# A graph network layer on one Trainium2 core: moving own sums, aggregate, turn and scatter between the gathered tiles on TensorE

## The reference

```python
w = jax.nn.relu(edgefeats @ fnet_w1 + fnet_b1) @ fnet_w2 + fnet_b2
W = w.reshape(-1, nc, nc)
deg = segment_sum(ones, edge_dst); inv_deg = 1.0 / maximum(deg, 1.0)
for _ in range(NREPEATS):                                  # 2
    xj = hx[edge_src]
    m = jnp.einsum('ei,eio->eo', xj, W)
    agg = jax.ops.segment_sum(m, edge_dst, num_segments=n_nodes) * inv_deg[:, None]
    hx = _gru_cell(agg, hx, ...)
x = _layernorm(x + hx)
```

## Time and profile before

| | |
|---|---|
| time, median of 3 runs | 6458.52 us (6440.29 to 6484.48) |
| profiled execution | 6451.35 us, its span 6449.0 us |
| mean granted clock of TensorE | 0.912 |
| PE busy | 85% of the span |
| DVE busy | 69% |
| POOL busy | 57% |
| ACT busy | 52% |

### The profile page before, as it was taken

One profiled execution on the slowest core, in us unless ns is written; L12 is line 12 of the kernel. 1 busy time (PEld: TensorE's weight loads), 2 busy tenths in 40 slices (PEclk: granted clock), 3 DMA queues, 4 the chain that ended last, 5 costly groups with the idle time before them and its releaser, 6 DMA issues.

```text
span 6449.0 us, 124558 instructions
## 1 busy us (share of the span) xinstructions
PE 5491.4 (85%) x41939; PEld 4396.8 (68%) x41940; DVE 4426.8 (69%) x5962; ACT 3328.3 (52%) x5306; POOL 3653.1 (57%) x3867
## 2 busy tenths in 40 slices
PE   2888888888888888888877888888988888888887
PEld 1766666676676776666646777767777767777775
DVE  3866666666666666666656777777777777777776
ACT  1555555555555555555434555555555555555553
POOL 6355555555555555555546555555555555555553
PEclk7998999998999999999988999999999999999998
DMA  5111111111111111111111111111111111111110
GB/s 119 40 45 36 51 36 51 36 51 36 42 44 41 46 38 49 36 51 36 48 51 31 31 43 37 37 43 31 43 43 31 43 31 43 43 31 43 43 31 21
DMA packets 190346, 270.76 MB, mean 42 GB/s; under 512 B 90119, under 2 KB 158234, under 8 KB 176887
## 3 DMA queue, kind: packets, MB, share of 16 engines
q1 hardware_dynamic: 58779, 224.93, 10.4%
q0 software_dynamic: 123168, 31.78, 4.7%
q10 hardware_dynamic: 7838, 6.41, 0.4%
HBM read 202.89 MB, written 54.94 MB: 40 GB/s over the span
## 4 chain that ended last, share of the span: by engine, by line
PE 67%; issue 13%; another core or an unknown queue 10%; ACT 5%; DVE 3%; DVEq 1%; ACTq 0%; DMA 0%; SPq 0%
PE ps_all L838 40%; PE ps_all L850 8%; PE ps_all L840 6%; PE ps_all L825 4%; ACT src_hot L700 3%; PE ps_all L873 3%; PE ps_all L894 2%; PE ps_all L864 2%; ACT src_hot L704 1%; DVE shared L1303 1%; DVE fan L1263 1%; PE ps_all L880 1%; DVE xg L1311 0%; PE ps_all L899 0%
## 5 line engine op out<-in xcount | busy, mean ns | idle before, releaser
L838 PE MATMUL ps_all<-parts,src_hot 128*128 128x448 f32 x14478 | 3672.3, 390 | 245.6 <-issue 97.2
L838 PEld LDWEIGHTS ps_all<-parts,src_hot 128*128 128x128 f32 x14478 | 2848.5, 199 | 639.3 <-issue 289.3
L628 POOL DMA_INDIRECT xg<-in_x,idx x1973 | 1868.6, 947 | 1435.5 <-issue 510.8
L628 POOL DMA_INDIRECT xg<-h_rows,idx x1876 | 1770.1, 944 | 1258.6 <-issue 474.8
L1303 DVE TENSOR_TENSOR shared<-ps_all,at_hot 128x448 f32<-128x448 f32 x2413 | 1406.7, 618 | 1499.8 <-PE ps_all L840 824.2
L700 ACT ACTIVATE src_hot<-keys,neg_key 128x384 fp32r<-128x384 int16 (+1 forms) x3088 | 1687.8, 619 | 1218.7 <-remote 578.5
L1311 DVE TENSOR_REDUCE xg<-shared 128x48 f32<-128x1344 f32 (+1 forms) x772 | 1244.3, 1612 | 82.0 <-DVE shared L1303 2.3
L704 ACT ACTIVATE src_hot<-src_hot 128x1536 fp32r<-128x1536 f32 (+1 forms) x772 | 1190.0, 1541 | 71.4
L1263 DVE TENSOR_TENSOR fan<-xg,ps_all 128x1280 f32<-128x1280 f32 x784 | 1159.5, 1479 | 40.7 <-issue 19.4
L850 PE MATMUL ps_all<-fan,h_sb 128*32 128x160 f32 x12544 | 742.5, 310 | 230.3 <-issue 209.8
L840 PE MATMUL ps_all<-parts,src_hot 128*128 128x448 f32 x2413 | 909.0, 377 | 13.1 <-issue 12.8
(11 more groups left out here) (134 smaller groups left out, 1368.3 us busy)
## 6 DMA issues: line engine op xcount, KB each, us to landing
keys<-key_d SPq DMA_DIRECT2D x98, 832.0 KB
h_d<-h_sb SPq DMA_DIRECT2D x49, 1056.0 KB
h_sb<-h_d SPq DMA_DIRECT2D x49, 1056.0 KB
xg<-in_x,idx POOLq DMA_INDIRECT x1973
xg<-h_rows,idx POOLq DMA_INDIRECT x1876
ef<-in_ef_t SPq DMA_DIRECT2D x49, 420.0 KB
acc_all<-agg_t SPq DMA_DIRECT2D x1, 3161.0 KB
idx<-in_src_tiles SPq DMA_DIRECT2D x98, 32.0 KB
```

What stands on the lines that cost most here:

```text
L628: pool.indirect_dma_start(out=xg[:, buf, at, 0:C], out_offset=None, in_=rows_of, in_offset=bass.IndirectOffsetOnAxis(ap=idx[:, buf, at:at ...
L838: pe.matmul(ps_g[j], src_hot[k % 2][:, kb, j * P:(j + 1) * P], parts[:, m * WHOLE + kb, :], start=(kb == 0 and m == 0), stop=False)
```

## The change

Nothing is added to or removed from the computation, and the streams of DVE, ACT, POOL and SP stay as they are. On TensorE `gather_rows` can now do part of its tiles. In each step, hidden and the first gathered tile come directly behind products. Then follow own sums, turn or scatter where the step has them, and the other gathered tiles behind these. In step 0 one tile stands between own sums and aggregate, and the last one behind aggregate.

```diff
-            def gather_rows(rnd, s, k):
+            def gather_rows(rnd, s, k, first=0, end=SLOTS):
 
-                for j, (n, _, _) in enumerate(pe_tiles(rnd, k)):
+                for j, (n, _, _) in list(enumerate(pe_tiles(rnd, k)))[first:end]:
...
+                        if rnd == 0 and not is_last(i):
+                            hidden(rnd, i + par, 1 - par, sup + 1, k)
+                        if not is_last(i):
+                            gather_rows(rnd, s + 1, k, 0, 1)
+                        elif SIDE_FROM <= k < HPS - 1:
+                            side_gates(rnd, k)
                         if not is_first(i, par):
                             if k == 0:
                                 pe.wait_ge(s_super, sup)
                                 own_sums(rnd, sup - 1, 1 - buf, 1)
+                                if not is_last(i):
+                                    gather_rows(rnd, s + 1, k, 1, 2)
                                 aggregate(sup - 1)
...
                             own_sums(rnd, sup, buf, 0)
-                        if rnd == 0 and not is_last(i):
-                            hidden(rnd, i + par, 1 - par, sup + 1, k)
                         if not is_last(i):
-                            gather_rows(rnd, s + 1, k)
-                        elif SIDE_FROM <= k < HPS - 1:
-                            side_gates(rnd, k)
+                            gather_rows(rnd, s + 1, k, 2 if k == 0 and not is_first(i, par) else 1)
```

## The result

The changed kernel takes 6764.22 us (median of 4, 6740.61 to 6769.57) against 6449.41 us of the kernel before in the same comparison: ratio 1.0477 with a 95% interval of 1.042 to 1.0534. The forecast was 6775. The total came out within 11 us; as the experiments show, its terms did not come out nearly so well, and two large errors cancelled.

A forecast was written before the change was run, and what follows sets the result against it. TensorE and POOL were taken to hand each other the step, small products waiting for POOL's DMA runs. Terms of 2.15 and 4.5 us a supertile gave 319 us over 48 supertiles, forecast 6775 us; range 6370 to 7100, likeliest 6600 to 6900.

The forecast's parts named there:

- The bound: TensorE and POOL hand each other the step; small products are handed over only between two runs of POOL's DMAs.
- Own sums in step 0: Behind a tile they are caught by POOL's run: +1.35 us a supertile in round 0, +2.9 in round 1.
- The tile ahead: Step 0: where products are late, a tile fills lost time: -1.0 us a supertile in round 0, -0.3 in round 1.
- Own sums in step 6: Caught by POOL's run too, with only two tiles behind: +0.4 us a supertile, bound 1.25 us per caught group.
- Aggregate: Step 0: it comes later, delaying ACT's copy and step 1's `src_hot`: +1.2 and +1.4 us a supertile, bounds 0 and 3.1.
- Turn and scatter: Issued behind a tile, so DVE's adding and ACT's copy start later: +0.2 and +0.1 us a supertile.
- The sum by rounds: All terms together: +2.15 us a supertile in round 0 and +4.5 in round 1, over 48 supertiles each.
- Faster by split bursts: Rival: halved bursts of small products end the stalls before own sums, at most 272.8 us gained (6185); chance 0.22.
- No change: Rival: POOL's hand-over paces the step, so moved stalls lengthen nothing: 6450 +- 60 us; chance 0.15.
- Borders at 164 us: Rival: each border pair between small and full-width products costs 0.31 us on TensorE, giving 6940 us; chance 0.08.
- Far slower: Rival: own sums caught in nearly every group as POOL's runs join, and the clock falls: 7130 us and above; chance 0.13.

The follow-up runs named there:

- e1: Kernel before, with only own sums of step 0 moved behind hidden and one gathered tile, aggregate directly behind them: 6513.36 us, ratio 1.0081, first chip.
- e10: Kernel before, with own sums of step 0 moved behind hidden and one tile in round 0 only: 6365.61 us, ratio 0.9866, first chip.
- e2: Kernel before, with only own sums of step 6 moved behind hidden and one gathered tile: 6608.03 us, ratio 1.0228, first chip.
- e3: Kernel before, with only aggregate moved behind hidden and two gathered tiles: 6623.49 us, ratio 1.0262, first chip.
- e12: Kernel before, with only aggregate moved and POOL's indirect DMAs replaced by plain ones of the same size: 5198.8 us, ratio 1.0415, third chip.
- e4: Kernel before, with only turn and scatter moved behind hidden and one gathered tile: 6462.77 us, ratio 1.0004, first chip.
- e9: Changed kernel with POOL's indirect DMAs replaced by plain ones of the same size, against the kernel before: 5282.73 us, ratio 1.0579, second chip.
- e11: Kernel before, own sums of step 0 moved in round 0 only, POOL's runs after own sums waiting for them: 5000.69 us, ratio 1.0014, second chip.

## Why the prediction was right, and where it was not

- **The bound.** That TensorE and POOL hand each other the step held on the first chip: POOL's waits for products, with those whose releaser isn't shown, are 308 us longer in a span that is 310 us longer. It was stated as a property of the small products and POOL's DMAs; the second chip shows that it is a property of the executions on the first chip, of which the profile of before could give no hint.
- **Own sums in step 0** (+1.35 and +2.9 us a supertile). The mechanism is right, its shares were not: products of step 0 were late in 40 of 41 supertiles of round 0, not in 70%, and newly held own sums were 5 of 41 there, not 30%. In round 1 they were 40 of 41, not 65%. The step's length was read from one step: 10.3 us, where the mean of round 0 is 14.2, so the 14.2 us that I forecast for the step after the change is what it took before. After it, it takes 10.2, and step 1 takes the time instead. With tile ahead and a part of aggregate's delay this step stood for 204 us in e1, and 52 to 55 were measured: -1.9 instead of +0.95 in round 0, +3.2 for +3.3 in round 1.
- **The tile ahead** (-1.0 and -0.3 us), named as the only gain, was under-sized in round 0. e10, in which hardly any own sums of round 0 are held, has it nearly alone: -1.3% of the kernel.
- **Own sums in step 6** (+0.4 us, 38 us in all) was the step that failed: e2 measured 147 to 150 us. The bound of 1.25 us was drawn inside the step. The cost fell two steps later, where POOL's runs join and catch own sums and aggregate of step 0, so that the step takes 19.4 us, a part of them at the lower clock. I had the row of such a joined run and used it as an upper bound of the wrong term.
- **Aggregate** (+1.2 and +1.4 us, 125 us in all): mechanism right, size 169 us alone on the first chip and 254 us on the third. "Less than half" of the shift was too little as a mean, and wrong by rounds: e3 has +0.1 us in round 0, where POOL's cycle takes the delay up, and +3.4 in round 1, where own sums of step 6 are also held in 38 of 41 supertiles. Where that cycle doesn't exist, e12 has +2.3 and +3.0 us, near the upper bound of 3.1.
- **Turn and scatter** (15 us): nothing measurable, +4 us.
- **The sum by rounds** came out as +2.0 and +4.6 us for +2.15 and +4.5. With e1 to e4 known this is luck: by them the terms should have come to about -1 and +12 us. In the whole, own sums of step 6 were 110 us too small and aggregate 44, own sums of step 0 and the tile ahead 150 us too large.
- **The rivals.** Faster by split bursts: excluded in both rounds as a whole; the "issue" time in front of own sums does fall, from 272.8 to 29.8 us (of their weights from 314.2 to 103.5), but DVE's wait at its copy of own sums grew, and "issue" grew in front of products, gathered tiles and aggregate. No change: excluded. Borders at 164 us: against it speak e4 on the first chip, for scatter alone, and e9, where at most 106 us can be borders. Far slower did not come on the whole, but its mechanism, joined runs and a clock at its lower level, is what made e2.

## What to carry to other kernels

Before a group of work is moved back on one engine, follow who copies its result and what stands behind that copy: here one copy of aggregate on ScalarE blocks the next step's `src_hot`, and that alone was three quarters of the cost on chips where nothing was held. Where two engines hand each other the step, a delay is not priced within its own step; look where the other engine's runs will join. Pieces of a change that are measured one by one can add up in total and still not explain it; compare them stage by stage. And a pattern of waits that only one chip shows is no law of the kernel: two edits that gained 1.3% and 0.9% there gained nothing together on the next.

## What the runs showed of the hardware that I had not expected

The same kernel took 6450 us on one chip, 4994 us on a second and 4992 on a third. POOL's DMAs are equally long in the traces of the first two (0.94 us, 1.25 us apart), and the mean granted clocks are 0.91 and, in e11, 0.99. On the first chip small products wait for the end of POOL's run of indirect DMAs: 512 of 784 groups of products in the kernel before, with a median of 2.7 us from the last product's start to its semaphore. In e11 on the second chip it is 2 of 784. Why the chips differ is open: the changed kernel with its indirect DMAs was run on neither of the other chips, nor plain DMAs on the first, and one of the two would be the next run to make.
